# The node features x of a graph attention layer, loaded in 32 transfers of 64 KB instead of 12 of 128 or 256 KB

## The reference

```python
s_i = emb @ attn[:d]
s_j = emb @ attn[d:]
e = jax.nn.leaky_relu(s_i + s_j.T, negative_slope=0.2)
e = e + jnp.where(adj > 0, jnp.float32(0.0), neg_inf)      # neg_inf = -1e9
alpha = jax.nn.softmax(e, axis=1)
return alpha @ emb
# and around it, with emb = x:
x = _layernorm(x + _L0_gnn_ref(adj, x, L0_gnn_attn), axis=-1)
```

## Time and profile before

| | |
|---|---|
| median of 3 runs | 254.55 us (253.83 to 254.62) |
| the profiled execution, time | 254.91 us |
| its span, first to last instruction | 253.0 us |
| PE busy | 243.4 us, 96% |
| DVE busy | 233.6 us, 92% |
| ACT busy | 175.5 us, 69% |
| POOL busy | 36.4 us, 14% |
| data read, mean rate over the span | 69.21 MB, 282 GB/s |

### The profile page before, as it was taken

How to read it: one execution, slowest core, us unless ns; L and a number is a source line. 1 busy time by engine, 2 the same in 40 slices (tenths; PEclk the granted TensorE clock), 3 DMA queues, 4 the chain that set the end, 5 groups by cost and what they waited for, 6 DMA issues and landing times.

```text
span 253.0 us, 2776 instructions
## 1 busy us (share of the span) xinstructions
PE 243.4 (96%) x801; PEld 128.1 (51%) x801; DVE 233.6 (92%) x383; ACT 175.5 (69%) x257; POOL 36.4 (14%) x74
## 2 busy tenths in 40 slices
PE   7999989989999999999999999999999999999991
PEld 6753434434444444444444444444444444699991
DVE  1979989989999999999999999999999999999834
ACT  1399999999499669396797568597966549504402
POOL 1000000000043004300240003300330003300612
PEclk9999999999999999999999999999999999999997
DMA  7999999999999999999999999999999980100001
GB/s 204 286 347 347 348 350 347 349 347 347 348 329 357 352 347 348 347 338 347 347 349 361 347 347 347 347 357 347 350 351 358 347 228 1 45 0 1 23 21 44
DMA packets 70258, 71.50 MB, mean 283 GB/s; under 512 B 2881, under 2 KB 68738, under 8 KB 70242
## 3 DMA queue, kind: packets, MB, share of 16 engines
q10 hardware_dynamic: 34592, 34.67, 44.1%
q1 hardware_dynamic: 34690, 34.74, 43.7%
q0 software_dynamic: 960, 1.90, 2.4%
HBM read 69.21 MB, written 2.10 MB: 282 GB/s over the span
## 4 chain that ended last, share of the span: by engine, by line
PE 87%; ACT 6%; ACTq 2%; DVE 2%; issue 2%; POOL 0%; POOLq 0%; DVEq 0%
PE psum L870 70%; PE psum L874 11%; ACT mask_bytes L416 2%; ACTq L271 2%; PE psum L826 2%; ACT xj L404 2%; ACT mask_bytes L422 1%; PE psum L811 1%; PE psum L866 1%; PE psum L837 1%; ACT adj_in L386 1%; DVE weights L725 1%; PE psum L814 0%; ACT adj_in L377 0%; PE psum L853 0%
## 5 line engine op out<-in xcount | busy, mean ns | idle before, releaser
L870 PE MATMUL psum<-weights,xj 128*128 128x512 f32 x448 | 194.5, 593 | 2.7 <-DVE weights L725 2.1
L725 DVE SCALAR_TENSOR_TENSOR weights<-q_row,r_j,mask_t 128x512 f32<-128x512 f32 x256 | 172.2, 740 | 0.3
L870 PEld LDWEIGHTS psum<-weights,xj 128*128 128x128 f32 x448 | 84.0, 190 | 108.8 <-issue 82.2
L422 ACT ACTIVATE mask_bytes<-adj_in 128x4096 uint8<-128x4096 int32 x27 | 97.4, 3613 | 22.3 <-DMA adj_in<-in_adj_dram 15.4
L611 DVE STREAM_TRANSPOSE mask_t<-mask_bytes 128x1024 uint32<-128x1024 uint32 x27 | 33.4, 1237 | 0.9 <-ACT mask_bytes L422 0.9
L874 PEld LDWEIGHTS psum<-xj,weights 128*128 128x128 f32 x256 | 28.8, 192 | 0.5 <-issue 0.5
L874 PE MATMUL psum<-xj,weights 128*128 128x128 f32 x256 | 28.9, 275 | 0.0
L342 POOL TENSOR_SCALAR neg_mean<-total 128x4 f32<-128x4 f32 x7 | 1.9, 277 | 157.7 <-ACT x_raw L435 157.7
L435 ACT ACTIVATE x_raw<-x_raw 128x128 f32<-128x128 f32 x28 | 8.2, 295 | 15.3 <-DVE x_raw L670 15.3
L351 POOL DMA_DIRECT2D out_dram<-x_raw x28 | 14.6, 526 | 18.8 <-ACT x_raw L449 18.7
L416 ACT ACTIVATE mask_bytes<-adj_in 128x2048 uint8<-128x2048 int32 x9 | 17.0, 1895 | 0.0
(11 more groups left out here) (65 smaller groups left out, 83.1 us busy)
## 6 DMA issues: line engine op xcount, KB each, us to landing
adj_in<-in_adj_dram ACTq DMA_DIRECT2D x64, 512.0 KB, 13.3
adj_in<-in_adj_dram SPq DMA_DIRECT2D x64, 512.0 KB, 14.0
out_dram<-x_raw POOLq DMA_DIRECT2D x28, 64.0 KB, 5.3
x_raw<-in_x_dram ACTq DMA_DIRECT2D x4, 128.0 KB, 3.3
x_raw<-in_x_dram SPq DMA_DIRECT2D x4, 128.0 KB, 3.5
x_raw<-in_x_dram ACTq DMA_DIRECT2D x2, 256.0 KB, 6.2
x_raw<-in_x_dram SPq DMA_DIRECT2D x2, 256.0 KB, 7.1
out_dram<-x_raw SPq DMA_DIRECT2D x2, 32.0 KB, 1.5
```

Source lines behind the costliest of these rows:

```text
L422: nc.scalar.activation(mask_bytes[:, g % BYTE_SLOTS, :, :, :], adj_in[:, g % ADJ_SLOTS, :, :, :], ACT.Sign).then_inc(bytes_ready, 1)
L725: nc.vector.scalar_tensor_tensor(weights[:, slot_of(n, c), :], q_row[:, n * BANK:(n + 1) * BANK], r_j[:, c:c + 1], mask_t[:, (n * PIECES + ...
L870: nc.tensor.matmul(banks[SUM_BANK[n % 2]][:, :], xj[:, c, :], weights[:, slot_of(n, c), :], start=(c == 0), stop=(c == CHUNKS - 1)).then_i ...
```

## The change

Each (quadrant, f) becomes a transfer of its own: 32 partitions with one run of 2 KB. SyncE and ScalarE each issue 16 transfers of x instead of 6. The bytes, the addresses on chip, the three parts, their order and the number of 2 KB runs (512 for each queue) are as before; within a part, all f of one quadrant now come before the next quadrant's, as before. The waits count 16 for each of the 8, 8 and 16 transfers of the parts (2, 2 and 4 for each quadrant). No wait is added.

```diff
+    LOADS = [(stop - first) // K for first, stop in zip(X_CUTS, X_CUTS[1:])]
...
             for q in quadrants:
-                queue.dma_start(x_raw[B * q:B * (q + 1), first:stop, :].rearrange("b (f k) d -> b f (k d)", k=K),
-                                x_v[q, :, first // K:stop // K, :]).then_inc(x_loaded[part], 16)
+                for f in range(first // K, stop // K):
+                    queue.dma_start(x_raw[B * q:B * (q + 1), f * K:(f + 1) * K, :].rearrange("b k d -> b (k d)"),
+                                    x_v[q, :, f, :]).then_inc(x_loaded[part], 16)
...
-            dve.wait_ge(x_loaded[0], 16 * Q)
+            dve.wait_ge(x_loaded[0], 16 * Q * LOADS[0])
             product_of(0)
             sum_products(0)
...
-                    pe.wait_ge(x_loaded[X_CUTS.index(m * K)], 16 * Q)
+                    pe.wait_ge(x_loaded[X_CUTS.index(m * K)], 16 * Q * LOADS[X_CUTS.index(m * K)])
```

More of the change, by code:

```diff
@@ L580, in _ @@
             dve.wait_ge(attn_j_ready, 1)
-            dve.wait_ge(x_loaded[0], 16 * Q)
+            dve.wait_ge(x_loaded[0], 16 * Q * LOADS[0])
             product_of(0)
             sum_products(0)
-            dve.wait_ge(x_loaded[1], 16 * Q)
+            dve.wait_ge(x_loaded[1], 16 * Q * LOADS[1])
             product_of(1)
             sum_products(1)
-            dve.wait_ge(x_loaded[2], 16 * Q)
+            dve.wait_ge(x_loaded[2], 16 * Q * LOADS[2])
             product_of(2)
```

## The result

The changed kernel takes 258.05 us in the median of 4 runs (257.07 to 258.30), the kernel before 254.59 (4 runs, 253.83 to 254.67). The ratio is 1.0136, 95% interval 1.0116 to 1.0156: slower by 3.5 us.

A forecast was written before the change was run, and what follows sets the result against it. TensorE's dense chain bounds the kernel, so lateness before about 57 us carries to the end. 2.3 (late copy) + 0.7 (pace) - 0.95 (stall given back) = +2.05 us, median 256.6; eight-in-ten range 254.8 to 258.6.

The forecast's parts named there:

- The issues: Prologue: ten more issues at 0.473 us cost ScalarE 4.73 us; after slack, its first copy makes s_i(0) 2.3 us late.
- The rival by which the issue costs by its runs: Issues of x: priced by descriptor, still 512 runs per queue, the change would be free; part of a 16% rival.
- TensorE's pace: s_i passes and turn_x(4) behind TensorE's 2.1 us gap: the fast pace may come later; +0.7 us taken, -0.7 to +1.4.
- the slow case: Four s_i passes at 0.85 take 3.4 us instead of 2.4, turn_x(4)'s transposes 0.85 instead of 0.45: +1.4 us.
- the forecast's doubt about that record: Around the s_i passes the granted clock reads 1.00 on both sides of the step, so the passes' pace decides; no size.
- The data: Loads of x and adj: x moved by about 9.5, adj up to 1 us later, pieces 0 and 1 hidden; no cost.
- What is given back: ScalarE's issue of part of piece 3 at 17.70 holds the scaling of x; that wait should go, -0.95 us.
- its low end: At ScalarE's issue of part of piece 3: as little as 0 gained if the queue is as full then.
- The slow pace to the maximum: TensorE stays slow until L853: +5.4 us, or 260; 257.8 if the step comes halfway; chance 15%.
- No change: Prologue: issues cost by runs or overlap, slack and ScalarE's stall absorb the delay; about 0, 254.5 us; chance 16%.
- faster: ScalarE's stall at 18.40 goes and the first copy comes by 8.9: up to -0.95, 253.6 us; chance 6%.
- the fourth: x at 347 GB/s would be moved 1.3 us earlier, worth nothing as TensorE awaits the copy; no chance of its own.

The follow-up runs named there:

- ScalarE alone late: Kernel before, plus ten unused 64-byte loads on ScalarE's queue behind its two transfers of piece 0 of adj; 256.51 us, ratio 1.0095.
- the busy TensorE: Changed kernel, plus 20 transposes of the identity into an unused PSUM bank before s_i(0); 257.91 us, ratio 1.0138 to the kernel before.
- the run with 14 loads: Kernel before, plus 14 loads of 64 bytes on each queue between x (12 transfers) and piece 0 of adj; 259.13 us, ratio 1.0192.
- both queues late by 10 loads: Kernel before, plus ten loads of 64 bytes on each queue between x (12 transfers) and piece 0 of adj; 256.96 us, ratio 1.0113.

## Why the prediction was right in sign and size, and where it was not

The forecast was 256.6, range 254.8 to 258.6, slower with 0.75; measured 258.05. In the profiled executions +2.05 was forecast and +3.21 came.

- **The issues.** Right. 0.473 us each was taken; sixteen took 7.52 us, 0.470 each. The first copy came at 10.98 (11.15), s_i(0) at 11.71 (11.8): +2.20 for +2.3. The rival by which the issue costs by its runs is out: the new issues took 0.44 us in the median on ScalarE, those with 64 and 128 rows 0.45.
- **TensorE's pace.** Right in kind, sized +0.7, measured +1.05 (from s_i(0) to copy 4: 3.07 before, 4.12 after). The four passes took 3.44, as the slow case had it. Two things differ. The gap was 3.17 us, not 2.1, since TensorE was at the fast pace from 5.46 in this execution and had turned its chunks by 8.5. And the granted clock does show the slow pace behind it: 0.73 in the mean of 12 to 18, against the forecast's doubt about that record. The Trainium skill's "TensorE: Matmul & The Clock Gate", Part 1, by which idle time brings back the slow clock, agrees with this trace (3.17 us idle, then 1.2 GHz); the execution with 2.05 us idle stayed at the fast pace.
- **The data.** This step failed: "With the stream up to 1 us later, from issues at 8.4 instead of 3.9 but behind x anyway, both stay hidden." The stream came 3.57 later, not 1. I had taken x and adj for one line of bytes that goes on at its full rate, in which the late issue only had to come before the bytes of x ran out, at about 9.5. What failed in it is the rate. From 2 to 10 us 0.2 MB fewer were moved than before (247 and 244 GB/s instead of 293 and 250), and from 10 to 16, where adj should have gone at 347, another 0.7 MB fewer (207, 197, 273 instead of 330, 346, 348). These 0.9 MB are 2.6 us at 348 GB/s; and, added up from the same stretches, 5.1 MB instead of 4.8 had been moved when piece 0 was complete, since more of the pieces behind it came along: another 1.0 us. So the slow start of adj is the larger part, and x held by its issues the smaller. Over all kernels this shows as a landing some 13 us behind the issue. Together with the forecast's own compute chain (+2.3 + 0.7) it would have been hidden at 1; at 3.57 it is the path.
- **What is given back.** Forecast -0.95, measured 0: ScalarE still idles 0.82 ahead of 22.48, because the issue that it stands behind took 1.41 us, nearly as long as before (1.54): the case that the forecast had named as its low end. With ScalarE alone late the issue took 0.59 and the stall shrank to 0.20. Taken out of the kernel before, the stall was worth 0.53 at the most.
- **The rivals.** The slow pace to the maximum did not come: TensorE was back at the fast pace by 15.2, its transposes of turn_x(4), (5) taking 1.08 for eight. No change and faster are out. Of the fourth, that x would move faster in one stretch, the opposite came: 247 and 244 GB/s, held by the issues, with the DMA engines at 0.86 and 0.84.

So the sum of the compute chain was 1.2 too small: +0.35 from the pace, +0.95 from what was not given back, -0.1 from the issues. That this chain (+3.25 at the maximum) and the data (+3.57) come out nearly the same is a coincidence, and it is luck that the forecast came as near as it did: a chain that it did not have would have made the time by itself. That the data hold the time when the compute chain is made earlier is shown by the busy TensorE. The other half, that the compute chain would hold it if the data were on time, is not shown for the whole: ScalarE alone late cost 2.4 us in the median, and its three slower runs (257.14 to 257.81) reach +3.1 to +3.7, but none of them was profiled.

**Open.** Why the first pieces of adj move slowly, above all when their issue comes late. The next fence is from the run with 14 loads, in which the last transfer of x, issued at 3.4, had landed by 10.5 (same columns as above; 347 GB/s is the rate of the settled stream):

```profile
8.00:10.00 2.00, 0.48 (x5) 0.24 (x3) 1.97 (x3) 0.13 (x1) 0.00 (x0) 1.00 0.67 184
10.00:12.00 2.00, 0.11 (x1) 0.14 (x2) 2.00 (x3) 1.99 (x3) 0.00 (x0) 1.00 0.95 213
12.00:14.00 2.00, 2.00 (x3) 0.83 (x4) 1.97 (x2) 1.22 (x3) 0.23 (x1) 0.54 1.09 211
```

The DMA engines are busy all the time from 12 to 14 and yet move 211 GB/s, so each packet takes longer. ScalarE's transfers behind piece 0 are not it, nor are small transfers of x needed for it, nor is it bound to the late issue: one execution with the issue at 3.57 had it mildly from 6 to 10 (250 GB/s), another did not (302). SyncE's transfers behind piece 0, and how the two queues share the engines, were not tested.

## What to carry to other kernels

A transfer costs its issuing engine nearly the same (here 0.47 us) whether it has 32 rows or 128, so cutting a load finer delays everything behind it in that stream: the engine's own computation, and the next stream of data. Count both from the issue, and do not count the bytes behind a late issue at the settled rate: here a stream that was issued 4.7 us later landed 3.6 us later, although its issue still came before the bytes ahead of it had all moved. When two chains are late side by side, an experiment on one of them shows nothing about it; take one away at a time and read who waits then.

## What was not expected of the hardware

- Piece 0 of adj (2 MB in four transfers) landed 12.8 to 14.0 us after its first issue in the seven kernels in which both queues had x alike and something waited for the piece, with 0.3 to 1.6 MB of x still ahead of it.
- Two executions with the same instructions up to 17 us had piece 0 at 17.46 and by 16.40, and moved 250 and 302 GB/s from 6 to 10.
- With 64 KB transfers on one queue and 512 KB transfers on the other, the small ones took up to 8.4 us (SyncE fine) and 9.2 us (ScalarE fine) from issue to landing; with both queues fine they took 4.2 at most.
- TensorE kept 2.4 GHz over 2.05 us of idle time in one execution (ScalarE late) and was at 1.2 GHz behind 3.17 in another (the change); with both queues late by 10 loads it had been idle for 2.33 and read 0.50 from 12 to 14.
